# Sixty-six bf16 products that nobody reads, put among the matmuls of six cross-attentions

## The reference

```python
qh = (q @ Wq + bq).reshape(B, LQ, 16, 8).transpose(0, 2, 1, 3)
kh = (k @ Wk + bk).reshape(B, 77, 16, 8).transpose(0, 2, 1, 3)
vh = (v @ Wv + bv).reshape(B, 77, 16, 8).transpose(0, 2, 1, 3)
attn = softmax(einsum('bhqd,bhkd->bhqk', qh, kh) / sqrt(8), axis=-1)
out = einsum('bhqk,bhkd->bhqd', attn, vh)
```

## Time and profile before

| | us |
|---|---|
| median of 3 runs | 1844.33 (1841.86 to 1844.79) |
| the profiled execution, its own time | 1841.01 |
| span of the profiled execution | 1839.3 |
| PE busy | 1573.7 (86%) |
| DVE busy | 876.1 (48%) |
| ACT busy | 738.2 (40%) |
| mean granted TensorE clock | 0.887 |

### The profile page before, as it was taken

How to read it: one execution, slowest core, us unless ns; L and a number is a source line. 1 busy time by engine, 2 the same in 40 slices (tenths; PEclk the granted TensorE clock), 3 DMA queues, 4 the chain that set the end, 5 groups by cost and what they waited for, 6 DMA issues and landing times.

```text
span 1839.3 us, 21926 instructions
## 1 busy us (share of the span) xinstructions
PE 1573.7 (86%) x8770; PEld 707.1 (38%) x8772; DVE 876.1 (48%) x1690; ACT 738.2 (40%) x1295; POOL 148.4 (8%) x209
## 2 busy tenths in 40 slices
PE   4947999879899989987659999788899989888397
PEld 2222323332344535732223332333444437533284
DVE  4184686253456343234555784433664442437212
ACT  2434555423545225242444554433454034253043
POOL 0000111100012000000000112000021000002321
PEclk9579899999999688987879999999997789899688
DMA  4000000000000100000000000000000100030241
GB/s 190 1 1 0 1 1 1 1 0 1 0 1 2 46 1 1 1 1 2 1 1 1 1 1 1 0 1 1 1 1 1 46 0 1 1 80 1 70 139 60
DMA packets 18105, 30.27 MB, mean 16 GB/s; under 512 B 4640, under 2 KB 12640, under 8 KB 17104
## 3 DMA queue, kind: packets, MB, share of 16 engines
q1 hardware_dynamic: 16752, 26.23, 4.5%
q0 software_dynamic: 1248, 2.59, 0.4%
HBM read 23.62 MB, written 5.19 MB: 16 GB/s over the span
## 4 chain that ended last, share of the span: by engine, by line
PE 77%; DVE 12%; ACT 7%; issue 2%; DMA 1%; POOL 1%; SPq 0%; POOLq 0%; DVEq 0%; ACTq 0%
PE ps L807 7%; PE ps L900 4%; PE ps L688 4%; PE ps L842 3%; PE ps L633 3%; PE ps L1350 3%; PE ps L1362 3%; PE ps L727 3%; PE ps L1030 3%; PE ps L951 3%; PE ps L931 2%; PE ps L855 2%; PE ps L1038 2%; PE ps L665 2%; PE ps L1265 2%
## 5 line engine op out<-in xcount | busy, mean ns | idle before, releaser
L2034 DVE TENSOR_REDUCE peak<-ps 128x1 f32<-128x512 f32 x256 | 163.9, 685 | 90.9 <-PE ps L807 89.2
L1665 ACT ACTIVATE big<-ps 128x512 f32<-128x512 f32 x256 | 140.7, 595 | 123.1 <-PE ps L834 121.3
L832 PE MATMUL ps<-qT,pp 32*128 32x512 f32 x512 | 161.1, 655 | 0.0
L807 PE MATMUL ps<-pp,qT 32*128 32x512 f32 x512 | 148.6, 662 | 1.4 <-ACT pp L1771 1.4
L1688 ACT ACTIVATE big<-ps 128x512 f32<-128x512 f32 (+3 forms) x256 | 101.2, 437 | 116.8 <-PE ps L931 115.8
L2079 DVE TENSOR_REDUCE crest<-ps 128x2 f32<-128x512 f32 (+3 forms) x128 | 104.8, 824 | 61.7 <-PE ps L906 61.5
L931 PE MATMUL ps<-qT,pp 32*128 32x384 f32 (+3 forms) x512 | 130.8, 521 | 2.3 <-ACT big L1688 1.8
L1604 ACT ACTIVATE big<-ps 77x1024 f32<-77x1024 f32 x96 | 93.7, 1017 | 91.9 <-PE ps L688 91.3
L1975 DVE TENSOR_REDUCE small<-ps 128x8 f32<-128x616 f32 x96 | 74.2, 796 | 94.1 <-PE ps L661 58.1
L900 PE MATMUL ps<-pp,qT 32*128 32x384 f32 (+3 forms) x512 | 105.4, 480 | 5.3 <-DVE crest L2079 2.7
L1584 ACT ACTIVATE sq<-ps 128x512 f32<-128x512 f32 x48 | 28.7, 597 | 182.5 <-PE ps L633 182.5
(11 more groups left out here) (480 smaller groups left out, 2726.3 us busy)
## 6 DMA issues: line engine op xcount, KB each, us to landing
big<-in_w SPq DMA_DIRECT2D x23, 256.0 KB, 3.3
pt<-in_l2w SPq DMA_DIRECT2D x2, 2048.0 KB, 7.8
w_l<-in_l SPq DMA_DIRECT2D x1, 3086.0 KB, 18.1
pp<-in_w SPq DMA_DIRECT2D x1, 2048.0 KB, 10.0
big<-by_expert SPq DMA_DIRECT2D x23, 66.0 KB, 1.9
by_expert<-cst SPq DMA_DIRECT2D x1, 1472.0 KB, 16.2
cst<-in_const SPq DMA_DIRECT2D x1, 1427.0 KB, 7.0
w_l<-in_l SPq DMA_DIRECT2D x1, 1218.0 KB, 9.1
```

Source lines behind the costliest of these rows:

```text
L807: pe.matmul(rbank(x), qT[at, u, k, 128 * i:128 * i + 128], keyT(u, k)[at, :], start=True, stop=True, tile_position=(32 * c, 0)).then_inc(* ...
L832: pe.matmul(tbank(y), keyT(u, k)[at, 128 * j:128 * j + 128], qT[at, u, k, :], start=True, stop=False, tile_position=(32 * c, 0))
L1665: A(prob(m)[:, TURN_OF[g], :], tbank(tplace(m, g)), ACT.Exp).then_inc(*SCALAR.did("a1", "exp", m, g))
L2034: v.tensor_reduce(peak[:, p // 4 % 2, i, c:c + 1], rbank(ring(p, c)), AX.X, ALU.max)\
```

## The change

A helper `unread(bank, n)` issues n matmuls of the full array, with the bf16 identity as the stationary operand and `w1q` as the moving one (512 columns), into a PSUM bank that the next real product overwrites. Nothing reads the result. It is called in four places of TensorE's `cross`:

- for `dh == 8`, one product ahead of each of `rowscores(0, 1)` to `rowscores(0, 7)`: seven;
- in all runs, three between the last row score of slot 0 and `turned(0)`, and two behind `turned(0)`;
- for `dh == 8`, two behind `turned(1)`, with a new wait for ACT's `kept 0, 0` ahead of them, since bank 0 holds the values of slot 0 until then.

That is 14 in each of the four runs with eight features per head and 5 in each of the two runs of a2, 66 in all.

```diff
+            def unread(bank, n):
+
+                for _ in range(n):
+                    pe.matmul(bank, identb[:], w1q[:], start=True, stop=True)
+
             def cross(tag, dh):
...
                 for a in range(8):
+                    if a and dh == 8:
+                        unread(PSB[0], 1)
                     rowscores(0, a)
+                unread(PSB[0], 3)
                 turned(0)
+                unread(PSB[0], 2)
                 for k in range(4):
                     if dh == 8:
                         for a in (2 * k, 2 * k + 1):
...
                 sums(0, 3)
                 values(0, 3)
                 turned(1)
+                if dh == 8:
+                    pe.wait_ge(*SCALAR[tag, "kept", 0, 0])
+                    unread(PSB[0], 2)
                 for k in range(4):
                     colscores4(1, k)
```

## The result

| | before | changed |
|---|---|---|
| median, us | 1843.0 (19 runs) | 1823.51 (19 runs) |
| lowest to highest | 1819.85 to 1862.0 | 1807.65 to 1832.93 |
| profiled execution, own time | 1841.01 | 1823.52 |
| span | 1839.3 | 1821.8 |
| mean granted clock | 0.887 | 0.903 |

The ratio changed to before is 0.9915, with a 95% interval of [0.9889, 0.9941]; it counts only runs within 1.5% of their kernel's fastest, which leaves out six of the 19 of before and none of the changed kernel. The change is faster by about 1%. The forecast was 1826 us, range 1814 to 1841.

The account below looks back on a forecast made before the run. PE sets the time in much of the program, in parts at 1.2 GHz. 1841.0 - 19.4 - 7.1 - 1.5 + 10.0 = 1823.0 us; with 3.3 us to the median, 1826 us, range 1814 to 1841.

Parts of the forecast that it names:

- Stretch A: Column scores behind `turned(0)`, four runs with eight features per head: 17.4 us each at full clock, saving 19.4 us.
- The straight line through the longest and the shortest: Stretch A's length against low-clock time, 0.38 us each: 17.1 us at zero, taken as 17.4 for PE waits.
- The lower bound of the saving: Stretch A in the four runs: 12.9 us saved if 19.02 us is already the floor.
- Stretch B: Stretch behind `turned(1)`: at full clock 22.54 becomes 15.41 us in one run, saving 7.1 us.
- a2: Attention with two runs: products around `turned(0)` save 1.5 us in the second run's stretch A, 0 in the first.
- The row scores: Seven products among slot 0's row scores: step 1.07 us on PE against DVE's 0.71, costing 10.0 us in four runs.
- stretch R: Row scores and their maxima ahead of `turned(0)`: 7.14 us before, about 9.6 us forecast.
- The 0.03 that I added for the identity's load: Part of the row-score step: 0.72 for the call, 0.32 for the product, 0.03 for the load, 1.07 us.
- The case of cheap row scores: Rival, chance 0.14: shape changes hide in the wait for DVE, stretch R costs 0 to 3 us, time 1818.
- The products around the transposes: Five around `turned(0)`, two behind `turned(1)`: all hidden in PE's gaps, cost 0; up to 0.2 us a run at low clock.
- the new wait: Wait for `kept 0, 0` behind `turned(1)`: ACT made it 4 us before, nobody is held, cost 0.
- The 3.3 us that I added for the median: Profiled execution of the kernel before lies 3.3 us under its runs' median, 1844.33; added to 1823.0 to give 1826.

Follow-up runs that it names:

- e3: Changed kernel with the seven products among the row scores on 32 of the array's rows, in the row scores' tile shape; 1819.75 us.
- e4: Changed kernel with three full-array products among the row scores, ahead of calls 2, 4 and 6, in place of seven; 1821.47 us.
- e8: Changed kernel with two full-array products ahead of each row score in place of one; 1831.03 us.
- e1: Changed kernel with only the seven products among the row scores, none around the turned maxima; 1844.21 us, ratio to before 1.0025.
- e11: e4's kernel without the two products behind `turned(1)` and their wait; 1817.53 us.
- e2: Changed kernel with only the products around the turned maxima, none among the row scores; 1821.06 us, ratio to before 0.9905.
- e6: e4's kernel run again, in one job with the changed kernel; 1818.75 us.
- e7: e3's kernel run again, in one job with the changed kernel; 1818.32 us.
- e5: The changed kernel run again, unaltered, for comparison within one job; 1826.78 us, ratio to before 0.9961.
- e10: e4's kernel plus products at two places of layer 1's attentions and four more at m = 27 and 28 of its causal attention; 1797.45 us.

## Why the prediction was right

In the six attentions the prediction was right step by step, and its mechanism as well. In two points, at the end of this section, it was helped by luck.

1. *Stretch A* was to be 17.4 us; it is 17.2. Saved: 10.5 + 5.6 + 2.4 + 1.8 = 20.3 us, forecast 19.4. The straight line through the longest and the shortest gave 17.1, and with my correction for waits it was 0.2 too much. The lower bound of the saving should have read 13.0 and not 12.9.
2. *Stretch B:* 7.1 forecast and measured.
3. *a2:* 1.5 forecast; 24.62 went to 23.11.
4. *The row scores* are where the forecast could have gone wrong by 10 us. The step was to be 1.07 us, it is 1.04; stretch R was to be about 9.6, it is 9.48; the price was to be 10.0, it is 9.3. It could be read from two rows of the kernel before in which one tile shape follows another: their 0.72 and 0.32 us make up the whole step. The 0.03 that I added for the identity's load is in no row, and the measured step has no room for it. The case of cheap row scores, to which I gave 0.14, is thereby out. e3, e4 and e8 show the cause: a product of another shape keeps the calls on either side of it from running side by side, and adds 0.32 us to each step of PE. Products in the row scores' own shape cost nothing. Three full ones between pairs of calls cost nothing either, though they change the shape too, since PE then stays ahead of DVE. A second product behind the first costs its columns alone.
5. *The products around the transposes* were hidden, as forecast, and e1 against the changed kernel shows that they do the work. e11 shows no effect of the two behind `turned(1)` and *the new wait* (6), beside three products among the row scores.

The rule of the Trainium skill on tiling modes ("TensorEngine Tiling (Array Packing)", Key Properties) agrees with these runs: a change of mode was paid. The price was the 0.1 us of the rows and not a whole tail of 0.18, which would have made the step 1.23. As to the other rule ("TensorE: Matmul & The Clock Gate", Part 4), that transposes do not count as busy in the same way: these runs show that a plain product by an identity is no such case, since e1 lacks the products around the transposes, and with them the clock stayed at 1.00 through the four stretches A where e1 lost it in each.

The sum of the steps is -19.6 us, the attentions took 19.9 less, and the span 17.5. The difference of 2.4 is in the rest of the program, which I had left at zero. It is not a cost of the change that the runs could show: that rest was 1548.6 in one trace and 1539.4 in the other of the same kernel. That the profiled execution came out at 1823.52, 0.5 us from my 1823.0, is luck: 1.9 us more were saved in the attentions than I forecast, and a rest that moves by 9 us happened to take 2.4 back. What I had not allowed for is how far executions of the kernel before differ: from three runs I read 1841.86 to 1844.79, and 19 went from 1819.85 to 1862.0. The 3.3 us that I added for the median stood on these three. Over all 19 the median is 1843.0, 2.0 us above the profiled execution, and in the changed kernel the median lies on it (1823.51 and 1823.52). That the 3.3 us put the forecast off by only 2.5 is luck too.

The weakest point is one that the sum does not show. The prediction named stretch R as a place where the clock is lost, and asked for the price of the seven products there but never for their worth. By e2 that is about 2 us in one trace against 9.3: without them the attentions are 6.7 us shorter, and with three of them, or seven in the row scores' own shape, the median is 8.0 and 8.5 us lower (e6, e7).

What stays open is why the clock was low for 48 us in the first run of the kernel before and only 7 to 17 us in the others, and which of a product's rows, columns and length hold it.

## What to carry to other kernels

A stretch in which PE is busy can still lose time to its clock: sum equal pieces of work apart, and where the lengths differ with PEclk while the other engines' busy times do not, the difference is what can be had. Fill the gap just ahead of the long stretch with products that nobody reads. In stretches where PE sets the pace or nearly does, keep such products in the tile shape of their neighbours or between groups that run side by side, and look for the place where the clock falls next: the largest gain of this study (19.5 us) came from four products there, behind six that by themselves had cost 2.6 us a turn.

## What was not expected of the hardware

- With the clock held, stretches of 7 to 23 us repeated to 0.01 us from turn to turn and run to run (17.19 or 17.20, 15.40 or 15.41). The scatter of this kernel on one core goes with the clock: of the 35 runs of before beside e5 the shortest (1821.73 us) had a mean granted clock of 0.897 and the longest (1861.26) 0.873. It is 42 us between 19 runs of before, 25 in the changed kernel, 2.7 in six runs of e10.
- Seven bf16 products on only 32 of the 128 rows, beside fp32 row scores on 32 or 64, went with a granted clock of 1.00 in eight runs of stretch R out of eight. Without them it was 0.87, 0.85 and 0.81 in three of four.
- Where the clock had already fallen in stretch R, it was back after 3.4, 3.4 and 6.8 us with five products around the transposes (e2), and after 47.8, 17.1 and 6.8 us in the kernel before. That the products did this is likely and not shown, with three falls of each kind.
